# Null scores of a routed attention with the roles of the two matmul operands swapped

## What is computed

```python
q = (xq @ w_q).reshape(b, -1, HEADS, DH).transpose(0, 2, 1, 3)     # 8 heads of 64
nk = broadcast(null_kv[0])          # one null key a head, the same for every sequence
k = concatenate([nk, k], axis=2)    # 1 + 1024 keys
v = concatenate([nv, v], axis=2)
sim = einsum('bhqd,bhkd->bhqk', q * DH ** -0.5, k)
attn = softmax(sim, axis=-1)
o = einsum('bhqk,bhkd->bhqd', attn, v)
return o @ w_out
```

## Time and profile before

| | |
|---|---|
| runs without the profiler | 4434.96 us median of 3 (4431.64 to 4438.22) |
| profiled execution, first to last instruction | 4433.8 us |
| TensorE matmul busy | 4163.1 us (94%) |
| VectorE busy | 2886.4 us (65%) |
| ScalarE busy | 1849.9 us (42%) |
| GpSimd busy | 875.9 us (20%) |
| mean granted TensorE clock | 0.961 of full speed |
| heavy attention | from about 2918 us to the end |

### The profile page before, as it was taken

One profiled execution on the slowest core, in us unless ns is written; L12 is line 12 of the kernel. 1 busy time (PEld: TensorE's weight loads), 2 busy tenths in 40 slices (PEclk: granted clock), 3 DMA queues, 4 the chain that ended last, 5 costly groups with the idle time before them and its releaser, 6 DMA issues. The chain is left out here.

```text
span 4433.8 us, 92598 instructions
## 1 busy us (share of the span) xinstructions
PE 4163.1 (94%) x37152; PEld 3493.5 (79%) x37152; DVE 2886.4 (65%) x5096; ACT 1849.9 (42%) x4838; POOL 875.9 (20%) x661
## 2 busy tenths in 40 slices
PE   5788879999999999999999999689999999999999
PEld 5777757888888888788888888577878878788777
DVE  9888867767676677755555666746464564645645
ACT  7444323434344444344444332325354453544534
POOL 0222102222222222212222222210110101101001
PEclk9999879999999999999999999879999999999999
DMA  8688742222222222211211211220220202112010
GB/s 309 165 234 232 211 141 79 92 82 90 82 92 80 91 82 92 65 58 59 68 58 61 65 58 48 90 57 6 51 49 15 53 8 51 37 24 52 12 41 13
DMA packets 341355, 360.63 MB, mean 81 GB/s; under 512 B 23104, under 2 KB 237376, under 8 KB 340928
## 3 DMA queue, kind: packets, MB, share of 16 engines
q1 hardware_dynamic: 262592, 287.52, 21.6%
q0 software_dynamic: 12288, 33.56, 3.6%
q10 hardware_dynamic: 66048, 33.56, 2.8%
HBM read 228.21 MB, written 76.02 MB: 69 GB/s over the span
## 5 line engine op out<-in xcount | busy, mean ns | idle before, releaser
L1683 POOL TENSOR_TENSOR l_prob<-l_prob,l_inv 128x768 f32<-128x768 f32 x256 | 389.6, 1543 | 1691.9 <-DVE l_inv L1640 1691.9
L1234 ACT ACTIVATE l_prob<-l_ps_s,l_neg_max 128x192 f32<-128x192 f32 x1024 | 419.7, 442 | 7.5 <-DVE l_neg_max L1616 7.3
L2294 DVE TENSOR_REDUCE h_neg_max<-h_ps_s 128x1 f32<-128x1024 f32 x256 | 312.9, 1222 | 167.2 <-PE h_ps_s L2080 165.5
L2215 ACT ACTIVATE h_prob<-h_ps_s,h_neg_max 128x1024 f32<-128x1024 f32 x256 | 285.3, 1115 | 279.5 <-DVE h_neg_max L2297 279.5
L1616 DVE TENSOR_REDUCE l_neg_max<-l_ps_s 128x4 f32<-128x768 f32 x256 | 233.2, 952 | 236.9 <-PE l_ps_s L1003 218.0
L2092 PE MATMUL h_ps_t<-ident,h_prob 128*128 128x128 f32 x2048 | 272.7, 276 | 14.6 <-ACT h_prob L2215 14.2
L2092 PEld LDWEIGHTS h_ps_t<-ident,h_prob 128*128 128x128 f32 x2048 | 228.2, 140 | 62.1 <-issue 27.7
L2351 DVE COPY h_probs_t<-h_ps_t 128x512 f32<-128x512 f32 x256 | 176.9, 691 | 124.7 <-PE h_ps_t L2092 123.8
L2104 PEld LDWEIGHTS h_ps_o<-h_probs_t,ahead_then_values 128*64 128x64 f32 x4096 | 220.9, 137 | 43.2 <-issue 37.0
L2104 PE MATMUL h_ps_o<-h_probs_t,ahead_then_values 128*64 128x128 f32 x4096 | 251.8, 276 | 0.0
L1234 ACT ACTIVATION_READ_ACCUMULATOR l_prob<-l_ps_s,l_neg_max 128x1 f32 x1024 | 235.5, 230 | 0.0
(11 more groups left out here) (385 smaller groups left out, 11136.5 us busy)
## 6 DMA issues: line engine op xcount, KB each, us to landing
toep_back<-taps_padded ACTq DMA_DIRECT2D x32, 1024.0 KB, 10.6
x<-xg SPq DMA_DIRECT2D x64, 512.0 KB, 8.7
l_xin<-x SPq DMA_DIRECT2D x128, 256.0 KB, 3.2
l_xres<-x SPq DMA_DIRECT2D x128, 256.0 KB, 3.1
l_val_side<-l_val SPq DMA_DIRECT2D x256, 128.0 KB, 3.1
out_dram<-l_res SPq DMA_DIRECT2D x128, 256.0 KB, 2.0
ahead_then_values<-x SPq DMA_DIRECT2D x126, 256.0 KB, 3.1
xin<-in_L_attn_x_dram SPq DMA_DIRECT2D x32, 768.0 KB, 6.4
```

Of the source, the lines that this page charges most:

```text
L1234: last = nc.scalar.activation(prob[t % 2][:, h, pair, :], ps_s[:, h, pair, BOTH], ACT.Exp, bias=neg_max[:, t % 2, h, pair:pair + 1], accum ...
L1683: nc.gpsimd.tensor_tensor(mine, mine, spread(inv[:, t % 2, h, :], [1, PAIRS], [0, WIN + P]), ALU.mult).then_inc(p_normed, 1)
L2215: nc.scalar.activation(prob[i % 2][:, :].rearrange("p (a k) -> p a k", a=2), ps_s[i % 2][:, :, :], ACT.Exp, bias=neg_max[:, qt % 2, h:h + ...
L2294: nc.vector.tensor_reduce(at, ps_s[i % 2][:, :, :].rearrange("p a k -> p (a k)"), AX_X, ALU.max, negate=True).then_inc(max_step, 1)
```

## The change

`null_scores` swaps the operands. `w["null_k"]` becomes [128, 8, 72], all zero but for one column of each head: that of head h stands in column h of its 72 (`null_column`). It is stationary; the 512 queries of the head stream. All 16 matmuls (8 heads, high and low part) add into one output [72, 512], whose row h is then the null score of head h for the 512 queries; rows 8 to 71 are zero. VectorE copies rows 0 to 7 to SBUF (`null_rows`); TensorE turns them back by four transposes [8, 128] to [128, 8], issued behind the first value projection of group 1; VectorE multiplies the 32 columns by -1 into `neg_null`. The waits for `doubled` are now one before each pair of heads.

```diff
+NULL_COLS = 72
@@ heavy_weights
+    def null_column(first, end):
+        return w["null_k"][first:end, :, :].rearrange("p h c -> p (h c)")[:, 0:(HEADS - 1) * (NULL_COLS + 1) + 1:NULL_COLS + 1]
-        nc.gpsimd.memset(w["null_k"][:, :, 1].bitcast(F32), 0.0).then_inc(zeroed, 1)
+        nc.gpsimd.memset(w["null_k"][:, :, :].rearrange("p h c -> p (h c)").bitcast(F32), 0.0).then_inc(zeroed, 1)
-        nc.gpsimd.tensor_tensor(w["null_k"][DH:P, :, 0], raw_null[DH:P, :], null_hi[DH:P, :].bitcast(F32),
+        nc.gpsimd.tensor_tensor(null_column(DH, P), raw_null[DH:P, :], null_hi[DH:P, :].bitcast(F32),
-        nc.scalar.activation(w["null_k"][0:DH, :, 0], raw_null[0:DH, :], ACT.Identity).then_inc(null_hi_made, 1)
+        nc.scalar.activation(null_column(0, DH), raw_null[0:DH, :], ACT.Identity).then_inc(null_hi_made, 1)
@@ heavy_phase
+        null_rows = sb("h_null_rows", [HEADS, NQ])
@@ TensorE
                 def null_scores(b):
-                    for a in range(PAIRS):
-                        pe.wait_ge(doubled[a], (b + 1) * 64)
+                    for h in range(HEADS):
+                        if h % 2 == 0:
+                            pe.wait_ge(doubled[h // 2], (b + 1) * 64)
+                        for q2 in (q2_hi, q2_lo):
+                            last = nc.tensor.matmul(ps_x[0:NULL_COLS, :], w["null_k"][:, h, :], q2[:, h, :],
+                                                    start=(h == 0 and q2 is q2_hi), stop=(h == HEADS - 1 and q2 is q2_lo))
+                    last.then_inc(null_made, 1)
+
+                def turn_null_rows(b):
+                    pe.wait_ge(null_rows_kept, b + 1)
                     for qt in range(QB):
-                        for h in range(HEADS):
-                            at = (qt * HEADS + h) * 2
-                            nc.tensor.matmul(ps_x[:, at:at + 2], q2_hi[:, h, qt * P:(qt + 1) * P], w["null_k"][:, h, :],
-                                             start=True, stop=False)
-                            last = nc.tensor.matmul(ps_x[:, at:at + 2], q2_lo[:, h, qt * P:(qt + 1) * P],
-                                                    w["null_k"][:, h, :], start=False, stop=True)
-                    last.then_inc(null_made, 1)
+                        last = nc.tensor.transpose(ps_x[:, qt * HEADS:(qt + 1) * HEADS], null_rows[:, qt * P:(qt + 1) * P],
+                                                   ident[0:HEADS, 0:HEADS])
+                    last.then_inc(null_rows_turned, 1)
@@
                             project_v(b, g, t)
+                            if t == 0 and g == 1:
+                                turn_null_rows(b)
@@ VectorE
                             v.wait_ge(null_made, b + 1)
-                            pairs = ps_x[:, 0:2 * STEPS].rearrange("p (i w) -> p i w", w=2)
-
-                            nc.vector.tensor_reduce(neg_null[:, :, :].rearrange("p q h -> p (q h)"), pairs, AX_X, ALU.add,
-                                                    negate=True).then_inc(null_kept, 1)
+                            nc.vector.tensor_copy(null_rows[:, :], ps_x[0:HEADS, :]).then_inc(null_rows_kept, 1)
+                            v.wait_ge(null_rows_turned, b + 1)
+                            nc.vector.tensor_scalar(neg_null[:, :, :].rearrange("p q h -> p (q h)"), ps_x[:, 0:STEPS], -1.0, None,
+                                                    ALU.mult).then_inc(null_kept, 1)
                             v.wait_ge(null_kept, b + 1)
@@
-        w |= {"out": sb("w_out_h", [P, KC, DIM]), "null_k": sb("w_null_k", [P, HEADS, 2], F32R)}
+        w |= {"out": sb("w_out_h", [P, KC, DIM]), "null_k": sb("w_null_k", [P, HEADS, NULL_COLS], F32R)}
```

More of the change, by code:

```diff
@@ L1940, in heavy_phase @@
         (normed, xt_turned, xt_hi_kept, xt_kept, projected, hi_kept, lo_kept, v_kept, null_made,
-         null_kept, s_made, max_step, max_made, exp_made, pt_made, pt_kept_dve, pt_kept_act, attended, gap_made,
+         null_rows_kept, null_rows_turned, null_kept, s_made, max_step, max_made, exp_made, pt_made, pt_kept_dve, pt_kept_act, attended, gap_made,
          null_exp_made, null_part_made, null_turned, null_t_kept, inv_step, inv_wide_made, inv_turned, o_read, att_kept, out_made, res_made) = (
@@ L1944, in heavy_phase @@
                  "normed xt_turned xt_hi_kept xt_kept projected hi_kept lo_kept v_kept null_made "
-                 "null_kept s_made max_step max_made exp_made pt_made pt_kept_dve pt_kept_act attended gap_made "
+                 "null_rows_kept null_rows_turned null_kept s_made max_step max_made exp_made pt_made pt_kept_dve pt_kept_act attended gap_made "
                  "null_exp_made null_part_made null_turned null_t_kept inv_step inv_wide_made inv_turned o_read att_kept out_made res_made").split())
```

## The result

The changed kernel takes 4364.7 us (median of 4 runs, 4361.7 to 4365.8) against 4434.3 us of the kernel before on the same chip: ratio 0.9845, 95% interval 0.9833 to 0.9856. Forecast were 4365.6 us.

A forecast was written before the change was run, and what follows sets the result against it. TensorE's own queue bounds the routed attention. New stretch 3.73 + 5.60 + 0.53 = 9.86 us against 18.54, gain 8.68, by eight 69.4: span 4433.8 to 4364.4, median 4365.6 us, range 4357 to 4382.

The forecast's parts named there:

- What bounds the stage: Routed attention: TensorE's own queue bounds it, waits about 27 of some 1480 us, so work removed shortens the end.
- The null matmuls: Null scores, per sequence: 64 matmuls of 10.63 us mean replaced by 16 at 0.2333 us, 3.73 us.
- The clock: Null scores and value projections: granted clock stays 1.00, so the 24 value matmuls cost 5.60 us instead of 7.91.
- the new stretch: First null-score matmul to next group's first row transpose: 9.86 us against 18.54, eight times, gain 69.4 us.
- Rival A: Same stretch: the clock stays low because its fall isn't the null scores' doing; gain 23 us, time 4412; chance 0.06.
- The split: Of the whole gain, 18.5 us is clock in the value projections, 51 us null scores with their turn back.
- The weight load rule: Old null matmuls: 107 ns per 128-column load whatever the clock; the 64 cost 6.8 us, time 4396; no chance given.
- The turn back: Four 8x512-strip transposes behind the first value projection: 0.45 + 0.08 = 0.53 us a sequence, bounds 0.36 and 1.0.
- VectorE's slack: Null-row copy done near 4.6 us, TensorE asks for it at 6.53: 1.9 us of slack.
- Rival B: Null matmuls: narrow stationary operands run as plain float, 0.885 us each; slower, 4449 us; chance 0.05.
- Rival C: Turn back stalls TensorE through late DVE or a long round trip: 1 to 3 us a sequence, 4374 to 4390; chance 0.07.
- 168 us between stretches: The seven stretches between the changed ones, 167.99 to 168.20 us long at clock 1.00, were to stay as before.

The follow-up runs named there:

- e7: Changed kernel without any null scores (null matmuls, copy and turn back gone, neg_null set to zero): 4327.0 us, ratio 0.9753 to the kernel before.
- e2: Kernel before with 128 moving columns instead of 2 in each of the 64 null matmuls, 126 of them zero: 4387.9 us, ratio 0.9891.
- e1: Kernel before with its 64 null matmuls cut into four pieces of 16, one behind each key projection of group 1: 4393.4 us, ratio 0.9904.
- e5: Changed kernel without the copy of the null rows and the four transposes, 128 stationary columns: 4357.5 us, ratio 0.9831 to the kernel before.
- e4: Changed kernel with the four transposes directly behind the null scores, so TensorE waits for VectorE's copy: 4371.4 us, ratio 0.9852 to the kernel before.

## Why the prediction was right

- *What bounds the stage* held: no wait of TensorE is new, and e7 shows that the work counts in full.
- *The null matmuls*: 3.73 us forecast, 3.68 measured.
- *The clock*: no drop was taken, and 1.00 was granted. The reason given, that the new stretch resembles its neighbours, is now shown from the other side: with two moving columns the clock falls in a block, with 128 it doesn't (e2), with two in four pieces it doesn't either (e1). Rival A, 0.06, falls. The Trainium skill (TensorE: Matmul & The Clock Gate, What's actually happening) says that activity releases the throttle. If busy records are taken for activity, the trace of the kernel before doesn't agree: they have no gap in the earlier trace rows, and the clock fell.
- *The split* was less well put. The text gave 18.5 us to the clock, that of the value projections, and 51 to the null scores. But of these the clock had its part too: at the high level the old null scores take 7.10 us (e2) and not 10.63, (10.63 - 7.10) x 8 = 28 us. So 28 + 19 = 47 of the 70.6 us of the stretches are clock, and 23.4 the swap. Most of the gain could be had without swapping anything. The 47 are those of the execution profiled, with five long stretches; with none or eight of them it would be 39 or 52.
- *The weight load rule*: the Trainium skill (TensorE: Matmul & The Clock Gate, LDWEIGHTS) puts a weight load at its columns divided by 1.2, in ns, which is 107 ns for 128. In e2, all at the high level, a matmul takes 0.111 us, near it; at the low level it takes 0.21, about twice as much.
- *The turn back*: 0.53 us forecast, 0.58 by the windows, 0.59 by leaving it out (e5). The row that the refill was taken from has 0.31 us between its starts, where the text says 0.32; the sum's 0.08 fits the 0.31.
- *VectorE's slack*: forecast to be done near 4.6 us, asked for at 6.53. The copy begins 3.88 us after the null scores and ends at 4.56; the transposes start at 6.49. Rival C priced: 0.86 us a sequence without the cover (e4).
- *Rival B*, the slower side, has no ground down to 8 columns. The 16 null matmuls took 3.68 us with 72 columns and 3.63 with 128 (e5), so the sentence that fewer columns can't lengthen them seems off by 0.05 us a sequence.
- *Luck*: the median fell by 69.6 us, and the forecast was 69.4. But the attention of the profiled pair gained 75.7 us, and the changed kernel started it 6.0 us later: two errors that cancel there. The first is 1.2 us more inside the stretches and 5.3 us more in the work between and behind them. The prediction had 168 us between stretches as before; they are 167.4, by a pace (below) that it gave nothing. The second is scatter of the phases ahead: over the 13 profiled kernels the start lies at 2927.9 to 2937.7 us. Whether some of it hangs on the kernel is open; the kernels with two moving columns and the others both have early and late ones.

## What to carry to other kernels

A block of matmuls with a long weight load and a very short moving side can cost more than its own time. Here the granted clock fell in the block and stayed low for the dense work behind it, while the records looked fully busy; so look at the granted clock of the windows behind such a block. Before rewriting it, try the two cheap cures that worked here: the block cut into pieces between dense work, or more moving columns of zeros (128 did it, 8 and 32 did nothing for the clock). Then swap the operands so that the long side streams, which here gave the last third of the gain. A result that comes out turned needs transposes. They cost 0.6 us a sequence here, and 0.9 more if no projection stood between VectorE's copy and them.

## What the runs showed of the hardware that I had not expected

**A pace beside the clock.** At a granted clock of 1.00, matmuls of 128x512 start 0.2333 us apart in some stretches and 0.2267 in others, 3%. In group 2 it was 8.40/36 = 0.2333 in the earlier trace rows; the same three projections take 8.17/36 = 0.2269 in the changed kernel. It was 0.2333 in the run with four pieces too, at a clock that never fell, and 0.2267 with 8, 32 and 128 moving columns, with and without a fall of the clock. So it doesn't go with the clock. It makes up the other half of what 8 and 32 moving columns gained in the attention.

It is tempting to put it down to the matmuls of two moving columns, which only the kernel before and the four pieces have. But both kernels are slower before the first of these matmuls has run. The last 24 key projection matmuls ahead of the very first null scores, before and in the changed kernel:

```profile
2950.42:2955.92 5.50, 5.50 (x26) 4.51 (x25) 3.85 (x7) 2.38 (x4) 0.00 (x0) 1.00 0.30 64
```

```profile
2956.69:2962.13 5.44, 5.44 (x26) 4.46 (x24) 3.85 (x7) 2.38 (x4) 0.00 (x0) 1.00 0.52 103
```

That is 0.229 us a start against 0.2267. In later sequences the kernel before again has 0.229 there, and in two of its eight key projections of group 2. So at least this part has another cause. One thing more sets these two kernels apart from all others: their tile of null keys is [128, 8, 2], 64 bytes in each partition, and 256 bytes or more elsewhere, which moves every tile allocated behind it. No run tells the two apart (the old matmuls with a larger tile, or the new ones with the small tile, would), so the cause stays open, and with it that of the step from 0.229 to 0.2333 behind the null scores.

**The fall comes 2.3 to 4.1 us into the block** in the kernel before, and 3.0 to 4.3 us in the runs with 8 and 32 columns, and the low level outlasts the block by 3.4 to 6.1 us of dense projections. The stretches come in two lengths in each kernel with a fall, 17.5 and 19.1 us. The low level itself, in the first and the second sequence of the kernel before, a short stretch and a long one:

```profile
2960.01:2970.25 10.24, 10.24 (x39) 9.27 (x40) 0.23 (x1) 0.00 (x0) 0.00 (x0) 0.50 0.00 0
3144.33:3157.98 13.65, 13.65 (x54) 12.49 (x54) 0.90 (x3) 0.00 (x0) 0.00 (x0) 0.50 0.00 1
```

In these three kernels every stretch in which the clock fell by 3.1 us into the block is a long one, and every one in which it fell at 3.5 us or later a short one. What sets the moment of the fall is not shown.
